# Splitting the next step's adapter matrix a1s right behind the last wide eviction, on GpSimd between its two x chunks of the second half

## The reference

```
cond(x) = (x @ B[id].T) @ A[id].T * 1.0
ffn(c)  = c @ W.T + b
        + sum_e alpha_e * 2 * ((c @ lora_A[e].T) @ lora_B[e].T)
alpha   = softmax_e(c @ router_W.T + router_b + log(prior))   # layer 0; layer 1 has no bias or prior
x = x + ffn0(cond0(x));   x = x + ffn1(cond1(x))
```

## Time and profile before

| what | value |
|---|---|
| time, median of 3 runs | 365.12 us (362.91 to 365.51) |
| span of the profiled execution, first to last instruction | 359.3 us |
| PE busy | 313.8 us (87%) |
| DVE, ACT, POOL busy | 242.6, 149.4, 89.6 us |
| DMA moved | 56.15 MB, mean 156 GB/s |
| granted TensorE clock, mean | 0.962 |

### The profile page before, as it was taken

How to read it: one execution, slowest core, us unless ns; L and a number is a source line. 1 busy time by engine, 2 the same in 40 slices (tenths; PEclk the granted TensorE clock), 3 DMA queues, 4 the chain that set the end, 5 groups by cost and what they waited for, 6 DMA issues and landing times.

```text
span 359.3 us, 6465 instructions
## 1 busy us (share of the span) xinstructions
PE 313.8 (87%) x2056; PEld 296.2 (82%) x2056; DVE 242.6 (68%) x496; ACT 149.4 (42%) x317; POOL 89.6 (25%) x61
## 2 busy tenths in 40 slices
PE   0936568889997999799979999999989998999975
PEld 0935568789997999699979998999989998999854
DVE  5914975788566864787397848784768566864564
ACT  5856833762065404650166206620573065402310
POOL 0014520193015500460026202530244015500000
PEclk9978858969999999999999999999999999999999
DMA  7899426712781078305950387029801880041005
GB/s 284 311 281 332 149 88 200 230 41 68 238 301 40 14 238 288 108 1 156 288 200 0 116 278 249 0 75 298 260 11 51 270 285 36 0 175 61 0 0 234
DMA packets 31524, 56.15 MB, mean 156 GB/s; under 512 B 3793, under 2 KB 21074, under 8 KB 31506
## 3 DMA queue, kind: packets, MB, share of 16 engines
q1 hardware_dynamic: 31506, 55.94, 46.7%
HBM read 39.15 MB, written 16.78 MB: 156 GB/s over the span
## 4 chain that ended last, share of the span: by engine, by line
issue 45%; PE 16%; POOL 14%; DVE 9%; SPq 6%; ACT 4%; DMA 4%; POOLq 0%; ACTq 0%; DVEq 0%
POOL xs_lo L909 12%; PE ps_d L318 4%; PE ps_d L320 3%; PE ps_d L319 3%; POOL a1s_lo L909 2%; DMA abraw<-ab_tab 2%; SPq L222 1%; DMA xraw<-x_in 1%; DVE w1s_lo L676 1%; SPq L233 1%; DVE xs_lo L676 1%; PE ps_h L325 1%; DVE bst_lo L676 1%; SPq L235 1%; ACT m1x_hi L512 1%
## 5 line engine op out<-in xcount | busy, mean ns | idle before, releaser
L909 POOL TENSOR_TENSOR xs_lo<-xraw,xs_hi 128x512 fp32r<-128x512 f32 x48 | 67.7, 1424 | 205.9 <-ACT xs_hi L512 205.9
L318 PE MATMUL ps_d<-w1s_hi,a1s_hi 128*128 128x384 f32 (+1 forms) x216 | 73.4, 340 | 9.5 <-DVE w1s_lo L676 9.5
L320 PE MATMUL ps_d<-w1s_hi,a1s_lo 128*128 128x384 f32 (+1 forms) x216 | 71.3, 330 | 0.0
L319 PE MATMUL ps_d<-w1s_lo,a1s_hi 128*128 128x384 f32 (+1 forms) x216 | 71.0, 329 | 0.0
L895 DVE SCALAR_TENSOR_TENSOR xraw<-ps_d,bsum,xraw 128x512 f32<-128x512 f32 x62 | 46.2, 750 | 26.1 <-PE ps_d L320 26.1
L318 PEld LDWEIGHTS ps_d<-w1s_hi,a1s_hi 128*128 128x128 f32 x216 | 42.3, 196 | 10.1 <-issue 8.4
L318 PE MATMUL ps_p<-xs_hi,bst_hi 128*128 128x256 f32 x128 | 39.4, 307 | 7.4 <-DVE xs_lo L676 3.6
L512 ACT ACTIVATE xs_hi<-xraw 128x512 fp32r<-128x512 f32 x64 | 37.3, 622 | 14.1 <-PE ps_p L320 8.5
L319 PEld LDWEIGHTS ps_d<-w1s_lo,a1s_hi 128*128 128x128 f32 x216 | 42.0, 195 | 0.0
L320 PEld LDWEIGHTS ps_d<-w1s_hi,a1s_lo 128*128 128x128 f32 x216 | 41.8, 194 | 0.0
L319 PE MATMUL ps_p<-xs_lo,bst_hi 128*128 128x256 f32 x128 | 37.9, 296 | 0.0
(11 more groups left out here) (154 smaller groups left out, 661.5 us busy)
## 6 DMA issues: line engine op xcount, KB each, us to landing
xraw<-x_in SPq DMA_DIRECT2D x32, 512.0 KB, 5.9
out<-xraw SPq DMA_DIRECT2D x32, 512.0 KB, 3.8
xraw<-w SPq DMA_DIRECT2D x16, 512.0 KB, 6.1
abraw<-ab_tab SPq DMA_DIRECT2D x64, 128.0 KB, 2.5
b0raw<-b_tab SPq DMA_DIRECT2D x64, 64.0 KB, 2.3
b0raw<-a SPq DMA_DIRECT2D x1, 512.0 KB, 3.6
lp<-exp SPq DMA_DIRECT2D x4, 69.0 KB, 7.3
cm<-exp_in SPq DMA_DIRECT2D x1, 144.0 KB, 6.6
```

What stands on the lines that cost most here:

```text
L318: pe.matmul(acc, lh, rh, start=first, stop=False, skip_group_check=True)
L319: pe.matmul(acc, lh, rl, start=False, stop=False, skip_group_check=True)
L320: return pe.matmul(acc, ll, rh, start=False, stop=final, skip_group_check=True)
L909: return pool.tensor_tensor(dst, whole, high.bitcast(F32), ALU.subtract)
```

## The change

The split of the next step's adapter matrix is moved forward on two engines. On ACT the copy `a1s_hi` goes from behind the exponential of softmax 1 to right behind the eviction of wide(2), in front of the first half-1 x chunk. On POOL `a1s_lo` goes from behind both half-1 x chunks to between them (0, then a1s, then 2). Everything else, the preamble's first split and SP's, PE's and DVE's orders included, is as it was.

```
@@ scalar, body
                 wide_high(2)
                 if not last:
+                    split_a(g + 1)
                     split_x(g + 1, 1 - par, 1, [0])
...
                     split_x(g + 1, 1 - par, 1, range(1, CH))
                 softmax_exp(1)
-                if not last:
-                    split_a(g + 1)
                 coef_high(1)
@@ gpsimd, body
                     split_x(g + 1, 1 - par, 0, range(CH))
-                    split_x(g + 1, 1 - par, 1, (0, 2))
+                    split_x(g + 1, 1 - par, 1, [0])
                     split_a(g + 1)
+                    split_x(g + 1, 1 - par, 1, [2])
```

## The result

The changed kernel takes 381.02 us (median of 4 runs, 380.76 to 384.12) against 364.27 us for the kernel before (median of 4 runs, 362.91 to 365.51). The ratio is 1.050, 95% interval [1.044, 1.057]; the two medians alone give 1.046. The sign was forecast, the size was not: 375.6 us is +2.9% on the 365.12 us that it was worked from. The measured 381.02 us stands just under the range's upper end of 382, but +5.0% on that base is 383.5 us, above it. The profiled execution took 380.76 us with a span of 378.7 us, 19.4 us more than the span of before.

The account below looks back on a forecast made before the run. The prediction took PE, busy 87% of the span, plus its gaps as the bound. 7 x 2.8 = 19.6 us of new gaps less 9.1 us closed gave +10.5 us on 365.12, so 375.6 us, range 366 to 382 us.

Parts of the forecast that it names:

- The sign: Whole kernel: slower by over 1%, chance 0.83; within 1%, 0.13; faster, 0.04.
- ACT's copy costs nothing: ACT, before the next xs_hi: the moved 1.04 us copy hides in 1.12 us of waiting for PE; cost 0.
- Gain of 9.1 us by earlier gathers: PE's turn 0 waits for the softmax, steps 1 to 6: gathers leave 2.75 us earlier and close them, 9.1 us.
- DVE held by POOL: Step boundary: DVE's k_lo second half waits for POOL's running a1s_lo, so route 1's second half starts 2.13 us later.
- Rival A: Step boundary: DVE isn't held, only POOL's order costs, 1.1 us in seven steps; 363.7 us, chance 0.1.
- 2.8 us at each boundary: Turn 1 on PE comes 2.6 to 3.1 us later, taken as 2.8, at seven boundaries: 19.6 us.
- the low case: Step boundary: k_lo 2 gets in before a1s_lo, DVE's xs_lo of chunk 1 is held instead; some 2.2 us.
- The sum: Whole kernel: 19.6 us of new gaps less 9.1 us of old gaps closed, +10.5 us, giving 375.6 us.
- main case: Whole kernel: DVE held and gathers earlier, +6.3 to +14.7 us, 371.4 to 379.8 us; chance 0.76.
- rival C: Head of each step: gathers land no earlier, so 19.6 us of new gaps stay; 384.7 us, chance 0.1.

Follow-up runs that it names:

- The ACT half alone: Changed kernel with a1s_hi early on ACT, but POOL's order as before (both x chunks, then a1s_lo): 365.79 us, 1.007 of the kernel before.
- hollow kernel: Changed kernel, but from the first boundary on POOL makes a1s_lo for 16 columns instead of 1024: 353.56 us, 0.976 of the kernel before.
- kernel with early gathers: Kernel before with only SP changed: eight b0raw gathers issued after the B splits, without waiting for a1s_lo: 351.83 us, 0.971 of the kernel before.
- memset run: The hollow kernel plus a POOL memset of the other 896 columns of a1s_lo behind the small subtraction: 354.07 us, 0.979 of the kernel before.
- filled kernel: Changed kernel with two redundant repeats of result tile 0's first three matmuls on PE before route 1's second half: 370.12 us, 1.024 of the kernel before.

## Why the prediction was half right, point by point

- **ACT's copy costs nothing**: right. PE's gap in front of route 1's first half is 0.31 us before and after. The ACT half alone even closed 7.7 of the 9.1 us of turn 0 gaps, as a1s_lo then starts right behind chunk 2.
- **Gain of 9.1 us by earlier gathers**: right in place and size. 10.2 - 1.3 = 8.9 us of PE's gaps closed, 8.3 us in the hollow kernel's time and 10.0 us in that of the kernel with early gathers. The shift itself was smaller than forecast: counted from turn 1 (160.13 before, 167.46 after), the last gather of step 2 leaves 2.1 us earlier (173.90 before, 179.12 after) and not 2.75, which still is enough.
- **DVE held by POOL**: right to some hundredths, as the turns were read off step 0: k_lo 2.47 us (some 2.5 forecast), DVE's xs_lo 1.65 us (1.66), chunk 2 finished after two more turns. Rival A falls. The statement of the Trainium skill in "GPSIMD Engine Reference", Key points, on DVE instructions with two SBUF inputs agrees with these rows: k_lo has two such inputs and took 2.47 us in place of 0.42. The memset run adds that POOL must be reading.
- **2.8 us at each boundary**: a little high. In the filled kernel, where the clock is full, turn 1 begins 162.03 - 155.62 = 6.4 us behind route 1 in step 2; before it was 160.13 - 156.30 = 3.8 us. So 2.6 us, and the steps say the same: 38.8 us filled, 36.2 us with early gathers and no held DVE. I had put 0.15 us from DVE's end to PE's start; it was 161.32 - 161.26 = 0.06 us. These 2.6 us hold for six boundaries; the seventh, behind step 0, took the turns of the low case (DVE's xs_lo held), which the prediction had named and counted like the others.
- **The sum**: this is the step that failed, by one missing term. I counted a stall as its own length ("The results behind it move with it, and no gap later in the step gives it back") at an unchanged clock. The rows of before gave reason to: a 2.32 us gap at turn 0 left the clock at 1.00. But behind the new gap in the middle of route 1 the clock was halved for 3 to 7 us at five of the six boundaries behind 90 us. That is 12.3 us by the spans (378.7 - 366.4) and about 10 us by the ratios, as much as the whole net of 10.5 us that I had forecast. Without it, the filled kernel is 7.1 us above the kernel before by the spans (366.4 - 359.3), and 8.3 us by the medians on one chip (370.12 - 361.85): inside my main case of +6.3 to +14.7 us.
- **The range**: its top stood for half of rival C. Rival C did not happen. A case "the clock falls" was not among the rivals; with what the runs show it would have added 10 to 12 us to the main case, 365.1 + 10.5 + 12 = 388 us at the most, so the range should have reached there. That 381.02 us lies so near the range's top is luck: the room up there was made for gathers that don't land earlier.

Open: what decides whether a gap lowers the clock. 2.32 us at turn 0 and 1.47 us at turn 1 did not. In the middle of route 1, 1.05 us did at three of six boundaries, 1.82 us at five of six in the changed kernel and at six of six in the one with early gathers. The gap in route 1 has 0.31 us of idle time and four short matmuls just ahead of it, and up to 0.26 us behind, so PE's work is thin on both sides; that this decides was not tested by itself. It can't be all: the gap of 2.05 us in front of chunk 2 has twelve 128x256 matmuls right ahead of it and lowered the clock at five of six boundaries, and the same gap at the same place lowers it in one step and not in the next.

## What to carry to other kernels

Price a new PE gap twice: its length, and a possible stretch at half clock behind it. Here those stretches were worth more than the gaps themselves, new less old, and two repeated products in the gap, which did nothing for the result, won it back. Before moving an elementwise instruction with two SBUF inputs within POOL's queue, list the two-input instructions that DVE will start while it runs: each was held to its end here. And where an order is changed to release a wait earlier, ask first whether the waiting queue needs to wait for it at all: here half of the gathers did not.

## What the runs showed of the hardware that I had not expected

- Filling 1.4 us of one gap a step was worth 10 to 12 us in the whole kernel, as the clock then did not fall at the boundaries (1.00 behind 90 us, against 0.95).
- A DVE instruction of 16 columns (0.17 us in step 0 of the kernel before) took 1.94 us beside a running two-input POOL instruction, so the hold does not scale with the size of DVE's instruction.
- POOL's memset of 128 x 896 took 0.84 us and did not hold two DVE instructions with two SBUF inputs (0.42 and 0.69 us, as usual).
